# The second system's 2 MB load issued in quarters inside the recurrence's first two blocks, its solver begun 12 half chunks later

## What is computed

```python
x = x + 0.5 * ffn(layernorm(x))        # a small feed-forward net
x = x + attn_block(layernorm(x))       # gated delta rule, then an MLP of 2048
x = x + 0.5 * ffn(layernorm(x))

def _step(Sm, inputs):                 # the delta rule: one token, per head
    q_t, k_t, v_t, beta_t = inputs
    Sk = einsum('bhde,bhe->bhd', Sm, k_t)
    delta = v_t - Sk
    Sm = Sm + beta_t[..., None] * einsum('bhd,bhe->bhde', delta, k_t)
    return Sm, einsum('bhde,bhe->bhd', Sm, q_t)
```

## Time and profile before

| | |
|---|---|
| median of 3 runs | 3170.09 us (3166.7 to 3174.82) |
| the profiled execution | 3168.27 us, span 3166.5 us |
| PE busy | 3037.5 us, 96% of the span |
| DVE busy | 1941.0 us, 61% |
| ACT busy | 1420.6 us, 45% |
| POOL busy | 1222.5 us, 39% |
| mean granted clock of PE | 0.979 |

### The profile page before, as it was taken

How to read it: one execution, slowest core, us unless ns; L and a number is a source line. 1 busy time by engine, 2 the same in 40 slices (tenths; PEclk the granted TensorE clock), 3 DMA queues, 4 the chain that set the end, 5 groups by cost and what they waited for, 6 DMA issues and landing times.

```text
span 3166.5 us, 148606 instructions
## 1 busy us (share of the span) xinstructions
PE 3037.5 (96%) x67876; PEld 2488.1 (79%) x67876; DVE 1941.0 (61%) x3190; ACT 1420.6 (45%) x3226; POOL 1222.5 (39%) x1225
## 2 busy tenths in 40 slices
PE   5999999999968999999999999999999999999998
PEld 4777777777757999999888787877778787777876
DVE  5888878878758999998513443444444344444434
ACT  5554545444413555555454433444443344444334
POOL 1446565655635877766311221112222112122211
PEclk8999999999978999999999999999999999999999
DMA  3545555554575777777661232222222222222220
GB/s 105 161 141 179 156 161 160 153 163 141 161 224 170 225 227 229 230 217 215 200 201 57 68 79 67 58 76 77 57 70 77 67 58 76 77 58 73 73 67 27
DMA packets 471354, 402.34 MB, mean 127 GB/s; under 512 B 68032, under 2 KB 391744, under 8 KB 471104
## 3 DMA queue, kind: packets, MB, share of 16 engines
q1 hardware_dynamic: 460960, 382.39, 41.5%
q10 hardware_dynamic: 10144, 16.63, 1.8%
HBM read 199.69 MB, written 153.09 MB: 111 GB/s over the span
## 4 chain that ended last, share of the span: by engine, by line
PE 83%; DVE 7%; issue 4%; SPq 3%; DMA 2%; ACT 1%; POOL 0%; DVEq 0%; ACTq 0%
PE bank L238 18%; PE bank L240 17%; PE bank L239 17%; PE bank L1280 14%; PE bank L1365 6%; SPq L1697 3%; PE bank L477 3%; PE bank L429 2%; DMA x2T<-HT 1%; PE bank L438 1%; PE bank L1769 1%; PE bank L421 1%; PE bank L1758 1%; PE bank L412 1%; DVE tmp L1527 1%
## 5 line engine op out<-in xcount | busy, mean ns | idle before, releaser
L2015 DVE TENSOR_TENSOR glo<-gl,gh 128x512 fp32r<-128x512 f32 x256 | 202.0, 789 | 702.5 <-ACT gh L1887 701.0
L1883 ACT ACTIVATE gl<-bank,b1m 128x512 f32<-128x512 f32 x256 | 176.3, 689 | 693.7 <-PE bank L240 693.7
L238 PE MATMUL bank<-h,w_hi 128*128 128x512 f32 x1024 | 404.8, 395 | 0.1
L240 PE MATMUL bank<-h,w_lo 128*128 128x512 f32 x1024 | 400.4, 391 | 0.0
L240 PE MATMUL bank<-w_hi,glo 128*128 128x512 f32 x1024 | 399.6, 390 | 0.0
L238 PE MATMUL bank<-w_hi,gh 128*128 128x512 f32 x1024 | 399.3, 390 | 0.0
L239 PE MATMUL bank<-h,w_hi 128*128 128x512 f32 x1024 | 398.8, 389 | 0.0
L239 PE MATMUL bank<-w_lo,gh 128*128 128x512 f32 x1024 | 398.3, 389 | 0.0
L1280 PE MATMUL bank<-ringA 32*32 32x32 f32 x16384 | 344.0, 197 | 12.9 <-issue 8.1
L1280 PEld LDWEIGHTS bank<-ringA 32*32 32x32 f32 x16384 | 271.7, 105 | 11.5 <-issue 6.0
L238 PEld LDWEIGHTS bank<-h,w_hi 128*128 128x128 f32 x1024 | 192.1, 188 | 67.6 <-issue 29.0
(11 more groups left out here) (195 smaller groups left out, 7284.2 us busy)
## 6 DMA issues: line engine op xcount, KB each, us to landing
ringB<-heads_scratch SPq DMA_DIRECT2D x256, 192.0 KB, 3.4
ringA<-heads_scratch SPq DMA_DIRECT2D x256, 128.0 KB, 2.6
x2T<-HT SPq DMA_DIRECT2D x480, 64.0 KB, 2.1
X<-in_L_attn_x SPq DMA_DIRECT2D x16, 1024.0 KB, 10.2
x_scratch<-X SPq DMA_DIRECT2D x16, 1024.0 KB, 4.2
heads_scratch<-vb SPq DMA_DIRECT2D x16, 1024.0 KB, 6.1
heads_scratch<-qk SPq DMA_DIRECT2D x16, 1024.0 KB, 7.2
heads_scratch<-kb SPq DMA_DIRECT2D x16, 1024.0 KB, 5.2
```

Of the source, the lines that this page charges most:

```text
L238: e.matmul(o, lhs[0], rhs[0], start=first, stop=False)
L240: return e.matmul(o, lhs[1], rhs[0], start=False, stop=last)
L1883: e.activation(ordered, made, ACT.Gelu_apprx_tanh, bias=b1m[:, m:m + 1]).then_inc(a_gl, 1)
L2015: e.tensor_tensor(gh[k][1][:, :], gl[k][:, :], gh[k][0][:, :], ALU.subtract).then_inc(v_gl, 1)
```

## The change

The four loads of system 1 leave the end of the projection. In the recurrence's first two blocks SP issues one quarter of them behind the ring loads of chunks 4, 5, 8 and 9. The solver's slots for system 1 begin at half chunk 12 (chunk 6) instead of 0 and end where they did, so its steps stand closer. All other systems keep their slots.

```diff
--- before.py
+++ after.py
@@ -59,6 +59,8 @@
 
 NG = 2 * GROUPS
 
+BEGIN1 = 12
+
 
 def solver_slots(systems):
 
@@ -73,7 +75,7 @@
             w = 3 * (CH - 1 - j) * j + 64
             steps += [("mul", j, w), ("add", j, w)]
         steps += [("back", n, turn) for n in range(GROUPS)]
-        begin, end = max(0, 2 * (NC * (s - 1) - 8)), 2 * (NC * s - 8)
+        begin, end = max(BEGIN1, 2 * (NC * (s - 1) - 8)), 2 * (NC * s - 8)
         share = sum(w for _, _, w in steps) / sum(room[half % 8] for half in range(begin, end - 1))
         credit, at = 0, 0
         for half in range(begin, end):
@@ -389,9 +391,6 @@
                     fill_rings()
                 store_v(t)
                 store_q(t)
-            e.wait_ge(p_proj, 13 * NT)
-            for quarter in range(4):
-                load_system(1, quarter)
             store_k(NT - 1)
             store_b(NT - 1)
             store_gram(NT - 1)
@@ -1216,11 +1215,17 @@
                 if c + 4 < CHUNKS:
                     load_a(c + 4)
                     load_b(c + 4)
+                if blk == 0:
+                    e.wait_ge(p_proj, 13 * NT)
+                if blk < 2:
+                    load_system(1, 2 * blk)
                 if blk >= 2:
                     store_z(blk - 2)
                 if c + 5 < CHUNKS:
                     load_a(c + 5)
                     load_b(c + 5)
+                if blk < 2:
+                    load_system(1, 2 * blk + 1)
                 if 8 <= c % NC < 24 and c // NC + 2 < NS:
                     load_system(c // NC + 2, c % NC // 4 - 2)
                 i = piece2(blk + 2)
```

## The result

| | before | changed |
|---|---|---|
| median of 6 runs | 3168.82 us | 3188.93 us |
| lowest and highest | 3166.7 to 3174.82 | 3184.17 to 3191.68 |
| span of the profiled execution | 3166.5 us | 3185.1 us |

The ratio is 1.0065, with a 95% interval of 1.0054 to 1.0076: the change makes the kernel about 20 us slower.

The account below looks back on a forecast made before the run. It took VectorE, without a gap from chunk 6 on, to hold TensorE in the middle stretch. Terms -2.5 + 19.4 + 0.7 + 0.8 = +18.4 us on 3168.27 gave 3186.7, plus 1.8 for the median 3188; range 3174 to 3197.

Parts of the forecast that it names:

- early gain: Chunks 0 to 5: without the load, TensorE's long idle pieces shrink; 2.5 us gained, bounds 0 and 10.
- The price of VectorE's work: From chunk 6 on: the whole solver stands where VectorE has no gap, 73.0 us of work; +19.4 us.
- The sign that TensorE would wait some 20 us more for `low`: Four blocks from chunk 6 on: TensorE waits for `low` some 20 us more, at a lower granted clock.
- The landing: Behind chunk 5: the last quarter lands in 5 us, just in time for `low(2)` at chunk 8, within a microsecond.
- The clock's return: End of the slow stretch: TensorE's granted clock has to come back to full; +0.8 us.
- The 0.7 us for `low(11)`: Behind chunk 22's `low`: an `add_out`, a back transpose and system 2's first turn stand before `low(11)`; +0.7 us.
- the 20.9 us: Chunk 6 on: VectorE's added work 19.4, the wait for `low(11)` 0.7 and the clock 0.8 us together.
- (1): Rival for chunks 0 to 5: the early stretch gains its full excess, 9.9 us; 3181 us, chance 0.10.
- (2): Rival for the middle stretch: VectorE and GpSimd exclude each other, 17.5 us more; 3205 us, chance 0.03.
- (3): Rival behind chunk 5: the last quarter lands late, at 10.8 us, so 5.8 us later; 3194 us, chance 0.07.
- (4): Rival for chunks 0 to 5: not slower, code refills stop holding TensorE, 24 us gained; 3167 us, chance 0.04.
- (5): Rival for the middle stretch: VectorE is not the holder, the solver fits in idle time; 3170 us, chance 0.03.

Follow-up runs that it names:

- e1: The kernel before with only system 1's solver begun at half chunk 12, the load left in its old place: 3186.2 us, ratio 1.005.
- e3: The kernel before with system 1's solver begun at half chunk 6, the load left in its old place: 3180.97 us, ratio 1.003.
- e9: The kernel before with the solver's credit in system 1's first 12 half chunks times 1.5, so more steps stand early: 3161.53 us, ratio 0.9982.
- e4: The kernel before with the solver's credit in system 1's first 12 half chunks doubled, so more steps stand early: 3159.89 us, ratio 0.9964.
- e8: The changed kernel with the last tile's stores of q, k and beta times k cut to 2 of 16 chunks: 3184.1 us, ratio 1.0049.
- e2: The changed kernel with all four quarters of the load issued in block 1: 3191.35 us, ratio 1.0065.
- e5: The changed kernel with GpSimd's 60 products and sums of system 1 cut to one element a partition: 3181.47 us, ratio 1.0038.
- e6: The changed kernel with VectorE's 60 products and sums of system 1 cut to one column in each of three groups: 3169.24 us, ratio 1.0.
- e10: The kernel of e4 (credit doubled, against the kernel before) run once more: 3159.93 us, ratio 0.9975.
- e7: The kernel before with the solver's credit in system 1's first 12 half chunks tripled: 3160.22 us, ratio 0.9974.

## Why the prediction was right, step by step

The time came out at 3188.93 us for a forecast of 3188 (its sum gives 3188.5). The place and the mechanism of the loss were right; that the time fits to 1 us is luck, since its errors cancel. The early gain was 3.8 us too high, which makes the forecast too low; the terms of the price together were 2.8 us too high, and a head start of 1.1 us of the profiled execution stood in no term, which makes it too high. The median of before also came out 1.3 us lower with more runs.

**The price of VectorE's work** held in its mechanism and nearly in its size. Forecast from the turns to the end of `low(10)`: 73.0 us; measured 972.52 to 1045.27, 72.75. The 60 products and sums took 53.02 us where I had taken 54 from between 50.7 and 55.2. That it is the solver's place and not the load's, e1 shows by itself (16.8 of the 18.1 us), and the doses of e3, e9 and e4 show it in both directions. The sign that TensorE would wait some 20 us more for `low` was put too high: it waited 14.1 more, and 4.0 went into a longer busy time.

**The landing** was mis-sized: I took 5 us and the turn began 3.92 us behind the issue, so 4.4 us behind chunk 5 instead of 5.8. It did fit under PE's output product and two chunks, as forecast: PE was busy without a gap from 974 to 981 us.

**The clock's return** was mis-sized: 0.8 us expected, nothing seen. The granted clock did fall (0.84 over the stretch), and PE's block stayed hidden under DVE's, but the row from 1050 us on has clock 1.00. The 0.7 us for `low(11)` was 0.5. Together the 20.9 us were 18.1.

**The early gain s** is the step that failed: 2.5 us forecast, and -1.3 measured from the last mask on (-0.1 to -3.3 by the spread of the profiles). My reason for the low end was right, since the pieces are long behind the stores (e8). That 2.5 us would still be left was wrong. The 0.5 MB of the third quarter lengthened a piece by 1.1 us, which I had named but not taken off, and e2, with no bulk load there at all, won only some 1.3 to 2.2 us in chunks 0 to 4.

**The rivals.** (1) is excluded by the early stretch itself and by e2. (2), exclusion of the two engines, would have needed a DVE sum well above a later system's 55; it was below it, and e5 puts POOL's whole price at 8.1 us for 60 instructions. The Trainium skill's rule on the shared port (SBUF — State Buffer, "Who interferes with whom") names the right pair, and the trace has its size here: 53.02 against 44.92 us, 18% more. Blocking for whole instructions, as the prediction reads the rule, does not fit: DVE's 60 took 53.02 us and POOL's 60 took 48.71 within some 73 us, so at least 28 us of them lay side by side. (3) did not occur: the last quarter landed within 3.92 us, though the ring load of chunk 9 had been issued 0.36 us ahead of it. (4) fell with the early gain. (5) is excluded by e6.

**Not foreseen:** the chain names POOL, with 31% and 29%, where I had said that DVE would hold the stretch alone. DVE and POOL run the system side by side, and POOL ended it 0.3 us behind DVE. The chain goes to whichever is last; e5 and e6 tell what each is worth.

**How far the early pieces are explained:** that DMA traffic lengthens them is shown by two interventions, the doses of the load and e8's stores. That they are refills of code rests on the count of packets and on a piece behind each 128 matmuls in the quiet part; no row names the packet that a piece waited for.

## What to carry to other kernels

Work of a helper engine that is spread over time has a price only where that engine is full, so look for the stretch in which it idles beside a slow main engine and put more of it there; here it was the very stretch from which the change took it, and doubling its share gained 0.25% to 0.36%, where the change, which empties it, lost 0.65%. A bulk load that seems to crowd a stretch is only one of its neighbours: before moving it, sum what else is in the queue. A wait of the main engine can cost more than itself: here, without its 5.9 us of waits, TensorE also needed 3.5 us less for its work, at a higher granted clock. And when the chain of waits names one of two engines that run side by side, cut the work of each in turn, since the chain gives all of it to the one that ended last by a fraction.

## What the runs showed of the hardware

The block of four chunks is not one constant. In e4 it took 10.50 us (7.56 and 2.94) from 981 to 1023 us and 10.6 to 10.9 later, at the same granted clock of 1.00 and with PE busy all of the time in both:

```profile
973.00:1023.00 50.00, 50.00 (x3864) 46.34 (x3865) 45.23 (x55) 26.57 (x113) 30.11 (x36) 1.00 0.78 240
1023.00:1066.00 43.00, 43.00 (x3126) 39.64 (x3116) 40.09 (x47) 22.91 (x95) 36.22 (x42) 1.00 0.68 209
```

e10 and e7 have the same two lengths. The longer block goes with the place in the program and not with the time: in the changed kernel the first three blocks behind the product of block 5, from 1049.80 us on, took 10.7, 10.8 and 10.9. The chunks' inverses come from DRAM at first and from `xt` from chunk 32 on, but e4's first ring load of the latter kind goes out at 1031.33, when the block that began at 1023.43 already took 10.6. POOL is busier later (36.22 of 43 us against 30.11 of 50). Neither was tried, and the cause stays open. It has no part in e4's gain, since the stretch that it gained in ends with the product of block 5.
